# Two expert expansions moved into the last attention step, and the numbers and gate of the last batch moved behind later expansions

## What is computed

```python
x = embeddings                                        # (8, 512, 128)
p = softmax(causal((x @ W_Q) @ (x @ W_K).T / sqrt(128)))
x = layernorm(x + p @ (x @ W_V))
logits = (x @ gate_w + gate_b) / 0.9                  # (8, 512, 8)
g = softmax over the two largest logits, 0 elsewhere
h = gelu(einsum('bsd,edf->bsef', x, w1) + b1)         # exact gelu
y = einsum('bse,bsed->bsd', g, einsum('bsef,efd->bsed', h, w2) + b2)
y = layernorm(y) * ln_g + ln_b
out = layernorm(x + y)
```

## Time and profile before

| | |
|---|---|
| median of 3 runs | 269.65 us (269.62 to 270.47) |
| span of the profiled execution | 269.3 us |
| the profiled execution's own time | not listed apart from the three runs; their median lies 0.35 us above its span |
| TensorE matmuls busy | 233.3 us, 87% of the span |
| ScalarE, VectorE, GpSimd busy | 179.3, 171.8, 142.7 us |
| contractions (L559) and expansions (L548) on TensorE | 78.6 and 76.4 us |

### The profile page before, as it was taken

One profiled execution on the slowest core, in us unless ns is written; L12 is line 12 of the kernel. 1 busy time (PEld: TensorE's weight loads), 2 busy tenths in 40 slices (PEclk: granted clock), 3 DMA queues, 4 the chain that ended last, 5 costly groups with the idle time before them and its releaser, 6 DMA issues.

```text
span 269.3 us, 7291 instructions
## 1 busy us (share of the span) xinstructions
PE 233.3 (87%) x1867; PEld 213.1 (79%) x1868; DVE 171.8 (64%) x952; ACT 179.3 (67%) x524; POOL 142.7 (53%) x165
## 2 busy tenths in 40 slices
PE   2798998999999877899999999999999999998000
PEld 2547786788788757899999999999999999998000
DVE  0044668688888886458832333355568999899854
ACT  2255766678676578788787565655655996689931
POOL 8300006547776777777877775456444545446400
PEclk9999999999999797999999999999999999999655
DMA  4999012123121553315567776758689676913193
GB/s 117 276 337 319 12 40 68 53 60 102 49 90 62 129 136 114 101 61 121 127 162 213 210 225 178 220 161 232 197 268 348 206 232 156 304 57 119 39 300 90
DMA packets 44800, 42.36 MB, mean 157 GB/s; under 512 B 5440, under 2 KB 33520, under 8 KB 44768
## 3 DMA queue, kind: packets, MB, share of 16 engines
q1 hardware_dynamic: 40448, 33.10, 44.0%
q0 software_dynamic: 4320, 8.92, 9.5%
HBM read 27.89 MB, written 12.01 MB: 148 GB/s over the span
## 4 chain that ended last, share of the span: by engine, by line
PE 51%; DVE 15%; DMA 9%; ACT 8%; issue 5%; SPq 4%; DVEq 3%; ACTq 1%; POOL 1%; POOLq 0%
PE bank L559 14%; PE bank L548 13%; PE bank L413 6%; DMA pair<-returned 5%; PE bank L440 4%; DMA returned<-x,slot_back 3%; PE bank L399 3%; ACT rows L623 2%; DVEq L1128 2%; PE bank L461 2%; PE bank L404 2%; DVE sum_stats L1067 2%; ACT probs L631 2%; PE bank L428 2%; SPq L296 2%
## 5 line engine op out<-in xcount | busy, mean ns | idle before, releaser
L694 ACT ACTIVATE h<-bank,b_cols 128x128 f32<-128x128 f32 x284 | 80.7, 372 | 39.1 <-PE bank L548 38.1
L1267 POOL DMA_INDIRECT returned<-x,slot_back x71 | 70.8, 998 | 52.3 <-DVE x L1048 45.0
L1262 POOL DMA_INDIRECT slots<-rows,slot_of x64 | 63.7, 996 | 57.3 <-DVE rows L916 39.0
L559 PE MATMUL bank<-w_all,h 128*128 x568 | 78.6, 282 | 0.0
L548 PE MATMUL bank<-slot_xT,w_now 128*128 128x128 f32 x568 | 76.4, 278 | 0.0
L548 PEld LDWEIGHTS bank<-slot_xT,w_now 128*128 128x128 f32 x568 | 70.5, 195 | 0.0
L559 PEld LDWEIGHTS bank<-w_all,h 128*128 128x128 f32 x568 | 69.0, 192 | 0.8
L822 DVE CAST slot_back<-slot_x 128x1 uint32<-128x1 f32 x71 | 10.4, 147 | 43.1 <-PE bank L548 43.0
L781 DVE TENSOR_REDUCE negmax<-bank 128x1 f32<-128x128 f32 (+3 forms) x32 | 14.7, 484 | 20.4 <-PE bank L414 20.0
L440 PEld LDWEIGHTS bank<-v,probsT 128*128 128x128 f32 x160 | 20.6, 200 | 5.7 <-issue 3.8
L1048 DVE TENSOR_SCALAR x<-bank,slot_gate 128x128 f32<-128x128 f32 x71 | 23.9, 340 | 0.0
(11 more groups left out here) (151 smaller groups left out, 301.6 us busy)
## 6 DMA issues: line engine op xcount, KB each, us to landing
w_now<-in_L_ffn_w_dram SPq DMA_DIRECT2D x47, 256.0 KB, 3.3
slot_x<-slots SPq DMA_DIRECT2D x71, 65.0 KB, 2.7
w_all<-in_L_ffn_w_dram SPq DMA_DIRECT2D x16, 256.0 KB, 5.8
pair<-returned SPq DMA_DIRECT2D x16, 256.0 KB, 3.1
x<-n_L_attn_embeddings_dram SPq DMA_DIRECT2D x8, 256.0 KB, 4.1
rows<-rows SPq DMA_DIRECT2D x8, 256.0 KB, 2.8
returned<-x,slot_back POOLq DMA_INDIRECT x71, 3.6
slots<-rows,slot_of POOLq DMA_INDIRECT x64, 2.3
```

The costliest lines, as they stand in the source:

```text
L559: m = nc.tensor.matmul(o, h[:, s % RING, c * P:(c + 1) * P], w2_c, start=False, stop=(c == FC - 1))
L694: m = nc.scalar.activation(h[:, s % RING, cols], bank_[:, cols], ACT.Gelu, bias=b1_cols[:, c:][:, bass.ds(first, 1)])
L1262: g_.indirect_dma_start(slots, bass.IndirectOffsetOnAxis(ap=slot_of[:, b, c:c + 1], axis=0), rows[:, k, b * TB + t, :], None).then_inc(dis ...
L1267: g_.indirect_dma_start(returned, bass.IndirectOffsetOnAxis(ap=slot_back[:, j:j + 1], axis=0), y[:, j % Y_RING, :], None).then_inc(y_retur ...
```

## The change

TensorE's last attention step becomes a function of its own. It transposes the first three slots before the second and third weighing, into bank A0 (`psT_of`), expands tiles 0 and 1 between the last weighing and the gate of batch 6, and transposes slots 3 and 4 at its end; `body(0)` starts with step 2. `prefix_sums(6)`, `transpose_xn(7)`, `gate(7)` and `prefix_sums(7)` go behind steps 3, 5, 6 and 7. ScalarE loads its expert numbers before the last step, takes the first two weights and gelu's table inside it, and puts `gate_tanh(6)`, `normalise_x(7)`, `copy_xnT(7)` and `gate_tanh(7)` behind the gelus of steps 2, 3, 4 and 7. VectorE copies slots 0 to 2 at the start of its last attention step, and slots 3 to 5 between root steps of batch 7's normalisation, each after `step_done` has reached 3. `norm_and_choose(8)` goes from step 3 to step 6, `route_link(7, 0..3)` to steps 8 and 9, `rest_table` to steps 10 to 15. SyncE loads the first four slots before it copies batch 5's rows, and reads the row numbers of the other four behind that.

```diff
...
     return ps_of_step[(s - AHEAD) % 4][:, 0:P]
+
+def psT_of(j, s):
+
+    return A0[:, j * P:(j + 1) * P] if isinstance(j, int) and j < AHEAD else psT(s)
 def psY(s):
...
     sp.dma_start(slots[REGION * E:SLOTS, :].rearrange("(j p) w -> p j w", p=P), empty[:, E:BLOCKS, :]).then_inc(emptied, 16)
-    for b in range(B - 2):
+    for b in range(B - 3):
         copy_rows(b)
     sp.wait_ge(numbers_ready, 1)
-    first_rows = tile_rows(0, UNROLL)
+    first_rows = tile_rows(0, AHEAD + 1)
     sp.wait_ge(dispatched[0], 16 * TOPK * FIRST * TB)
     for s, at in enumerate(first_rows):
+        load_slots(s, at)
+    copy_rows(B - 3)
+    for s, at in enumerate(tile_rows(AHEAD + 1, UNROLL - AHEAD - 1), AHEAD + 1):
         if s == AHEAD + 1:
...
             pe.wait_ge(y_ready, i * UNROLL + (s - AHEAD - LAG - 3))
-        return nc.tensor.transpose(psT(s), slot_x[:, s, 0:D], ident[:])
+        return nc.tensor.transpose(psT_of(i if not isinstance(i, int) else i * UNROLL + s, s), slot_x[:, s, 0:D], ident[:])
     def step(b):
...
-        if b == B - 1:
-            pe.wait_ge(v_ready, B)
-            pe.wait_ge(pT_ready, B * UNITS)
-            for s in range(AHEAD):
-                transpose_slots(0, s).then_inc(first_psum, 1)
...
+
+    def last_step():
+
+        b = B - 1
+        transpose_probs(b, 0)
+        transpose_probs(b, 1)
+        weigh_values(b, 0)
+        transpose_probs(b, 2)
+        pe.wait_ge(v_ready, B)
+        for s in range(AHEAD):
+            transpose_slots(0, s).then_inc(first_psum, 1)
+        prefix_sums(b - 2)
+        weigh_values(b, 1)
+        weigh_values(b, 2)
+        expand(0, 0, False)
+        transpose_xn(b - 1)
+        expand(0, 1, False)
+        gate(b - 1)
+        pe.wait_ge(attn_read, B)
+        pe.wait_ge(slotT_ready, AHEAD)
+        transpose_slots(0, AHEAD)
+        transpose_slots(0, AHEAD + 1)
...
+    FIRST_EXPANDED = 2
+
     def body(i, first=False, late=False, last=False):
...
         e = expert_numbers(i * UNROLL, tiles)
-        for s in range(tiles):
+        for s in range(FIRST_EXPANDED if first else 0, tiles):
             if s + AHEAD < tiles:
...
             expand(i, s, late)
-            if first and s == 0:
+            if first and s == 3:
                 prefix_sums(B - 2)
-            if first and s == 2:
+            if first and s == 5:
                 transpose_xn(B - 1)
-            if first and s == 3:
+            if first and s == 6:
                 gate(B - 1)
-            if first and s == 5:
+            if first and s == 7:
                 prefix_sums(B - 1)
+    for b in range(B - 1):
+        step(b)
+    pe.wait_ge(ew_loaded, 16 * 2 * E)
+    pe.wait_ge(const_ready, NCONST)
+    pe.wait_ge(bias_ready, 5)
+    pe.wait_ge(numbers_ready, 1)
+    last_step()
     body(0, first=True)
...
+
+    def last_step(e):
+
+        b = B - 1
+        copy_probsT(b, 0)
+        copy_probsT(b, 1)
+        take_w1(0, e[0])
+        nc.scalar.activation(unused[:], ones[:, 0:1], ACT.Gelu)
+        copy_probsT(b, 2)
+        gate_tanh(b - 2)
+        take_w1(1, e[1])
+        normalise_x(b - 1)
+        copy_xnT(b - 1)
     act.wait_ge(ones_ready, 1)
...
     exponentials(0)
-    for b in range(B):
+    for b in range(B - 1):
         step(b)
...
         m.then_inc(done, 1)
-    def body(i, first=False, last=False):
+    def body(i, e=None, last=False):
+        first = e is not None
         tiles = LAST if last else UNROLL
...
         n = tiles + W1_AHEAD if not isinstance(i, int) or i < BOUND - 1 else tiles
-        e = expert_numbers(i * UNROLL + LAG, n)
+        e = e or expert_numbers(i * UNROLL + LAG, n)
         for s in range(tiles):
...
             gelu(i * UNROLL + s, s, act.snap(e[s] * FC))
-            if first and s == 0:
+            if first and s == 2:
+                gate_tanh(B - 2)
+            if first and s == 3:
                 normalise_x(B - 1)
-            if first and s == 2:
+            if first and s == 4:
                 copy_xnT(B - 1)
-            if first and s == 4:
+            if first and s == 7:
                 gate_tanh(B - 1)
...
     act.wait_ge(numbers_ready, 1)
-    for s, e in enumerate(expert_numbers(LAG, W1_AHEAD)):
-        take_w1(s, e)
-    nc.scalar.activation(unused[:], ones[:, 0:1], ACT.Gelu)
-    gate_tanh(B - 2)
-    body(0, first=True)
+    first_experts = expert_numbers(LAG, UNROLL + W1_AHEAD)
+    last_step(first_experts)
+    body(0, first_experts)
     with act.Fori(1, BOUND - 1) as i:
...
         if isinstance(j, int) and j < AHEAD:
-            dve.wait_ge(first_psum, j + 1)
+            dve.wait_ge(first_psum, AHEAD)
+        elif isinstance(j, int) and j < 2 * AHEAD:
+            dve.wait_ge(step_done, AHEAD)
         else:
...
         vec.tensor_copy(slot_gate[:, j % (2 * UNROLL):j % (2 * UNROLL) + 1], slot_x[:, s % UNROLL, GATE:BACK]).then_inc(slot_read, 1)
-        vec.tensor_copy(slot_xT[:, s % RING, :], psT(s)).then_inc(slotT_ready, 1)
-
-    def norm_and_choose(b, norm=True, choose=True, route=None, table=False):
+        vec.tensor_copy(slot_xT[:, s % RING, :], psT_of(j, s)).then_inc(slotT_ready, 1)
+
+    def norm_and_choose(b, norm=True, choose=True, route=None, table=False, slots=None):
         c = b - 1
...
                 rsqrt_step(i, rstd[:], var[:], square[:])
+                if slots and i in slots:
+                    copy_slots(slots[i], slots[i])
             dve.drain()
...
     def step(b):
+        if b == B - 1:
+            for s in range(AHEAD):
+                copy_slots(s, s)
         for u in range(UNITS):
...
             norm_and_choose(1, norm=False)
-        if b == B - 1:
-            for s in range(AHEAD):
-                copy_slots(s, s)
-        norm_and_choose(b, choose=b > 1, route=0 if b == 1 else None, table=b - 2 == FIRST - 1)
+        norm_and_choose(b, choose=b > 1, route=0 if b == 1 else None, table=b - 2 == FIRST - 1,
+                        slots={2: AHEAD, 4: AHEAD + 1, 6: AHEAD + 2} if b == B - 1 else None)
     def split_biases():
...
         for s in range(LAST if last else UNROLL):
-            if not last or s + AHEAD < LAST:
+            if (not last or s + AHEAD < LAST) and not (first and s < AHEAD):
                 copy_slots(i * UNROLL + s + AHEAD, s + AHEAD)
...
                 weigh(i - 1, s - LAG + UNROLL)
-            if first and s == 3:
+            if first and s == 6:
                 norm_and_choose(B, norm=False)
-            if first and s in (6, 7):
-                for q in (2 * s - 12, 2 * s - 11):
+            if i == 1 and s in (0, 1):
+                for q in (2 * s, 2 * s + 1):
                     dve.drain()
                     route_link(B - 1, q)
-            if isinstance(i, int) and i == 1:
-                for q in ((0, 1, 2, 3), (4, 5), (6, 7), (8,), (9,), (10, 11), (), ())[s]:
+            if i == 1:
+                for q in ((), (), (0, 1, 2, 3), (4, 5), (6, 7), (8,), (9,), (10, 11))[s]:
                     dve.drain()
```

More of the change, by code:

```diff
@@ L479, in transpose_slots @@
                     pe.wait_ge(y_ready, i * UNROLL + (s - AHEAD - LAG - 3))
-                return nc.tensor.transpose(psT(s), slot_x[:, s, 0:D], ident[:])
+                return nc.tensor.transpose(psT_of(i if not isinstance(i, int) else i * UNROLL + s, s), slot_x[:, s, 0:D], ident[:])
             def step(b):
-                if b < B - 1:
-                    transpose_x(b + 1)
+                transpose_x(b + 1)
                 transpose_probs(b, 0)
                 transpose_probs(b, 1)
-                if b < B - 1:
-                    project_g(b + 1)
+                project_g(b + 1)
                 if b == 2:
@@ L494, in step @@
                     prefix_sums(b - 2)
-                if b < B - 1:
-                    scores(b + 1)
+                scores(b + 1)
                 weigh_values(b, 1)
                 weigh_values(b, 2)
-                if b == B - 1:
-                    pe.wait_ge(v_ready, B)
-                    pe.wait_ge(pT_ready, B * UNITS)
-                    for s in range(AHEAD):
-                        transpose_slots(0, s).then_inc(first_psum, 1)
                 if b:
                     transpose_xn(b - 1)
-                if b < B - 1:
-                    project_v(b + 1)
+                project_v(b + 1)
                 if b:
                     gate(b - 1)
+            def last_step():
[18 more added lines that the diff above has]
+                transpose_slots(0, AHEAD + 1)
             pe.wait_ge(const_ready, FIRST_CONST)
@@ L645, in step @@
             def step(b):
-                if b < B - 1:
-                    copy_xT(b + 1)
+                copy_xT(b + 1)
                 copy_probsT(b, 0)
@@ L651, in step @@
                     gate_tanh(0)
-                if b < B - 1:
-                    copy_g(b + 1)
+                copy_g(b + 1)
                 if b > 2:
@@ L658, in step @@
                     normalise_x(b - 1)
-                if b < B - 1:
```

(7 more changed lines are left out.)

## The result

The change makes the kernel faster: 267.96 us (median of 15 runs, 266.52 to 270.00) against 270.47 us for the kernel before (15 runs, 269.44 to 274.08). The ratio is 0.9908 with a 95% interval of 0.9886 to 0.9930, that is 0.9% or 2.5 us. The sign is the forecast one, the size is not: 4.25 us were forecast, and 267.96 lies above the range, which ended at 267.2.

A forecast was written before the change was run, and what follows sets the result against it. It took TensorE's pace to bound the expert stage and a relay between engines to delay its start. Step 8 sooner (-4.6) plus slot stall (+0.3) gave -4.3 us on a 269.3 span, 0.35 added: 265.4, range 264.6 to 267.2.

The forecast's parts named there:

- ScalarE's part: Last attention step: weights and gelu's table moved earlier cost 0, with a cover of 0.2 us before batch 6's normalisation.
- From there TensorE has work in line: TensorE from expansion 3 to step 8: steps follow without gaps, step 8 begins at 113.4 against 118.00, 4.6 us gained.
- Moved numbers and pads: Pads' numbers two steps later delay SyncE's loads of slots 16 to 23: 0.3 us of stall, bounds 0 and 0.6.
- The next slots do not add to it: Slots behind slot 16 add no stall: an issue takes 0.33 us, a slot and a pad together less than a step.
- L: Follow-up theory, not forecast: contraction 3 to 4 loses time because loop register loads stand behind the last prefix sums' wait.
- the sum's own terms: The parts added up for the whole kernel: -4.6 at step 8 and +0.3 of slot stall; chance of the sum 0.55.
- (a): Clock falls to 0.50 in the new gap on TensorE: 266.7 with one stretch (chance 0.24), 268.4 with two (0.07).
- (b): Gelu's table load holds ScalarE another 1.28 us before the third copy of probabilities: 265.9, chance 0.04.
- (c): Another engine or the returns set the pace behind step 8, so the gain is lost: 269.65, chance 0.04.
- (d): VectorE's copy 3 waits for a late expansion 2 and holds up what is queued behind it: 270.5, chance 0.06.

The follow-up runs named there:

- small parts undone: Changed kernel with SyncE copying batch 5's rows first again and gelu's table loaded behind `copy_xnT(6)` again: 267.59 us, ratio 0.9876.
- only written out: Changed kernel with TensorE's `body(1)` written out instead of looped, last prefix sums left where the change put them: 268.80 us, one run.
- second body written out: Changed kernel with TensorE's steps 8 to 15 written out instead of looped and the last prefix sums behind step 8: 266.47 us, ratio 0.9874.
- numbers ahead: Changed kernel with `body(1)` written out, prefix sums unmoved, and the experts' numbers of steps 8 to 15 loaded behind step 6: 265.72 us, one run.
- the single edits: Changed kernel with either pads' numbers copied in step 8 (266.43 us) or TensorE's steps 8 to 15 unlooped and last prefix sums behind step 8 (266.47 us).
- both edits: Changed kernel with pads' numbers copied in step 8, TensorE's steps 8 to 15 unlooped and last prefix sums behind step 8: 265.31 us, ratio 0.9827.
- the sooner copy 3: On top of both edits, VectorE copies slots 3, 4 and 5 earlier in the last batch's normalisation: 264.74 us, ratio 0.9770.

## Why the prediction missed

**Up to contraction 0 it was right.** With 0.99 us added: copies at 94.55 (forecast 94.6), logits at 99.17 (99.0), copy 3 at 101.91 (101.81), expansion 3 at 102.37 (102.3) behind 1.60 us of idle (1.3), contraction 0 at 103.69 (103.6). ScalarE's part cost nothing, and expansions 0 and 1 went into gaps. Two of its sums are off in the second digit (97.1 and 1.82 make 98.92, not 98.95; 101.81 and 0.4 make 102.2, not 102.3), which changed nothing. It held up to the last prefix sums: 113.10 with the 0.99 added, where 113.2 was forecast.

**The step that failed first** is in the paragraph "From there TensorE has work in line": "a wait of 0.4; with 0.2 of sums step 8 begins at 113.4". The transpose that opens step 8 came at 114.18 with the 0.99 added. The wait and the sums measured 0.50 together, inside the 0.6 for them; what was put at nothing, without a reason, is what follows them in the queue. TensorE's queue enters its loop there, and the loop's numbers are only fetched once the wait is over (112.3 behind 112.11; fetched ahead, contraction 4 comes 0.7 us sooner). In the kernel before the same fetch ran below other work (116.2), and the earlier trace rows do not show it. Forecast for this passage 0.6 us, measured 1.64. The gain at contraction 4 was 3.53 us instead of 4.6.

**The second** is "Moved numbers and pads". The mechanism was right, and it was weighed: the pads' numbers come two steps later and the loads of slots 16 to 23 stand behind them. The term was mis-sized: 0.3 of stall with bounds of 0 and 0.6, where 1.87 was measured. Slot 16 itself was just in time (issued at 121.50, transposed at 123.60 without a wait). What fell is "The next slots do not add to it". The issues were as close as I had them (1.13 us for a slot and a pad), but the landings were not the 1.9 to 2.7 us of the earlier trace rows: slot 18's took 4.96 us. It had 4.0 us, from its issue at 123.77 to the end of expansion 14 (126.84 + 0.9), and was 1 us late. An upper bound drawn from the landings of a quieter stretch and from a median was no bound here.

**Together.** In the two traces, -4.6 + 0.3 = -4.3 became -3.4 + 1.9 = -1.5 at contraction 13, and the spans differ by 2.2 because the execution after had 0.99 us of luck before the change and lost 0.3 behind contraction 13. The medians say -2.5, but the stall changes between executions. Five traces have the late numbers and SyncE's order of the kernel after: the kernel after, small parts undone, only written out, second body written out, numbers ahead. From 9 to 13 they lose 1.87, 1.62, 0.96, 0.10 and 0.08 us, and by the landing events that the traces keep, slot 18 landed 4.96, 4.65, 4.48, 2.28 and 2.95 us after its issue. So the late order takes the slack, and a slow landing then makes the stall. The two traces with little stall, inside the forecast's bounds, are the two in which most of *L*'s loss was gone. The two losses may therefore not be independent; five traces do not settle it. By the medians the single edits give 1.53 and 1.49 us and both together 2.65, less than the sum.

With both losses taken away the gain over the kernel before is 1.7% (1.2 to 2.2), where 1.6% had been forecast for the change. With six runs the intervals of the single edits overlap the kernel after's. That each one removes its loss is shown by the traces; that both together shorten the time is shown by the interval of both edits, which ends at 0.9877 where the kernel after's begins at 0.9886.

**The base.** I took the median of three runs, 269.65, as 0.35 us above the profiled span. Every run here lies 1.8 us above its span, so that span belongs to an execution near 271.1, and fifteen runs have their median at 270.47. The forecast of 265.4 was 0.8 us too low for this alone. With that base the range would have ended at 268.0 and held 267.96; the gain would still have been 2.5 us where 4.25 was forecast.

**The rivals.** None of the four is what happened; the losses lay in the sum's own terms. (a), the clock, did not happen in this trace: 1.00 through the whole stage, although TensorE sat idle for 1.60 us in it; the narrow gate and the gaps there were not followed by the lower level. The warning of the Trainium skill, TensorE: Matmul & The Clock Gate, section HAM oscillation, about pauses between bursts of matmuls did not come true in this place; with the pads' numbers one step later still it did, at 0.50 from 128.50, behind a wait of 1.87 us. What the lower level would have cost behind expansion 3, no run shows; further back in the stage it cost nothing (14.81 with and without it). (b): no second wait beside the table's load; its 1.28 us end at 92.00 and the next rows follow at 92.02 and 92.13. The drain of about 1.38 us that the Trainium skill, ScalarE: Activation LUTs, section What ACT_TABLE_LOAD costs, puts beside a load is again not in the trace. (c): the end does follow, with losses of some tenths. (d): copy 3 did not wait.

**What stays open.** Why slot 18's landing took 4.96 us. Pads, slots and scatters move at the same time, and two of GpSimd's scatters there take 2.34 and 2.40 us instead of 0.96. But the trace before has two such scatters as well, 1.76 and 2.41 us, and by its landing events slots 16 to 23 landed after 1.85 to 3.95 us, slot 18 after 2.74. So slow scatters beside the loads are not enough to explain it. And of the 1.08 us of the sooner copy 3, most does not reach the end in its profile: from contraction 60 to 70 TensorE takes 17.93 us there against 16.61 with both edits alone, and ScalarE waits 1.31 us for VectorE's part of the output (at 231.75) before it takes the gelus behind it. Whether that comes again, no run tested.

## What to carry to other kernels

When work with a wait is moved to another place in an engine's queue, look at what comes next in that queue, register loads and a loop's entry included: they cost nothing as long as they run below other work, and their full length behind a wait. When a change eats the slack of a transfer, bound its landing by the slowest landings on record and not by a median, and do so for each transfer of the queue: here the first was in time and the third was not. When a version made worse loses what was expected, look in its trace for where it lost it: here part of it was the clock. And take the base from the profiled execution's own time.

## What the runs showed of the hardware

- A register load on TensorE's queue took 0.60 to 1.17 us in these traces. When it stood behind a semaphore wait, the matmuls behind it came about 0.7 us later than with the load ahead of the wait; the profile then named as releaser VectorE's scaling, which was not the cause.
- A slot load of 65 KB landed 1.9 us after its issue in a quiet stretch. Beside pad writes and scatters the same load, that of slot 18, took 2.28 to 4.96 us in five executions.
- The lower level of the clock (0.50) came in different places in two executions of the same kernel (twice 3.41 us, and once, 0.51 over 6.90 us) without changing the stage's length by more than 0.01 us. Behind a wait of 1.87 us, in a stage where TensorE sets the pace, it made a contraction take 2.07 us instead of 1.11.
